# Attention stage of a two-layer tower: positional products copied out by ScalarE, and the score maximum of heads 4 to 7 moved into the exponential's bias

## The reference, cut to what matters

```python
# fourth block: 8 heads of 8 columns, per sequence
patch_score = softmax(einsum('bhnd,bhmd->bhnm', q, k) * hd**-0.5)
pos_score = softmax(rel @ Wpos.T + bpos)            # 8 x 128 x 128, the same for every sequence
g = sigmoid(gating)                                 # one number per head
attn = (1 - g) * patch_score + g * pos_score
attn = attn / attn.sum(-1)
h = h + (einsum('bhnm,bhmd->bhnd', attn, v) @ Wproj.T + bproj)
# fifth block: top-2 of 8 experts, softmax over the two logits
logits = xn @ Wr + br
y = sum_e w[e] * (gelu(xn @ W1[e] + b1[e]) @ W2[e] + b2[e])
```

## Time and profile before

| what | value |
|---|---|
| median of 3 runs | 781.05 us (781.04 to 781.59) |
| profiled execution, its own time | 780.1 us |
| its span | 778.4 us |
| granted TensorE clock, mean over the span | 0.899 of full |
| busy in the span: TensorE / VectorE / ScalarE | 81% / 61% / 35% |
| attention loop, first scores to first `expert_up` | 596.7 to 697.8 us |

### The profile page before, as it was taken

One profiled execution on the slowest core, in us unless ns is written; L12 is line 12 of the kernel. 1 busy time (PEld: TensorE's weight loads), 2 busy tenths in 40 slices (PEclk: granted clock), 3 DMA queues, 4 the chain that ended last, 5 costly groups with the idle time before them and its releaser, 6 DMA issues.

```text
span 778.4 us, 12091 instructions
## 1 busy us (share of the span) xinstructions
PE 630.4 (81%) x4557; PEld 483.8 (62%) x4557; DVE 476.8 (61%) x1164; ACT 272.2 (35%) x463; POOL 358.5 (46%) x406
## 2 busy tenths in 40 slices
PE   6779999999986637776877886459997779898996
PEld 3547767785565526666766765425776567774666
DVE  3775344247666757899889999844333746555513
ACT  0034454428965501110000000055332536645440
POOL 1576233218026666897888995134542200000324
PEclk9999999998988957899999999668995889898998
DMA  7000000000003330000000000000000000000000
GB/s 230 0 1 1 1 1 1 0 1 1 0 23 75 73 71 1 1 1 0 2 0 1 1 1 1 0 1 1 1 1 1 1 1 2 1 2 0 8 8 13
DMA packets 9689, 10.33 MB, mean 13 GB/s; under 512 B 5792, under 2 KB 8544, under 8 KB 9376
## 3 DMA queue, kind: packets, MB, share of 16 engines
q1 hardware_dynamic: 7584, 7.90, 3.7%
q0 software_dynamic: 2048, 1.68, 1.1%
HBM read 5.70 MB, written 0.52 MB: 8 GB/s over the span
## 4 chain that ended last, share of the span: by engine, by line
PE 53%; DVE 30%; issue 4%; POOL 4%; ACT 4%; DMA 3%; SPq 2%; DVEq 0%; POOLq 0%; ACTq 0%
PE bank L1242 8%; PE bank L992 7%; DVE features L1671 7%; PE bank L980 6%; DVE bank L1705 5%; DVE features L1694 5%; PE bank L1258 4%; PE bank L1260 4%; PE bank L1069 3%; PE bank L1029 2%; POOL rstd L336 2%; PE bank L1318 2%; DMA coefs<-xs 2%; PE bank L1038 2%; SPq L373 2%
## 5 line engine op out<-in xcount | busy, mean ns | idle before, releaser
L1069 PE MATMUL bank<-ident,features 128*128 128x128 f32 x920 | 126.6, 296 | 66.0 <-DVE features L1671 47.7
L1069 PEld LDWEIGHTS bank<-ident,features 128*128 128x128 f32 x920 | 113.4, 154 | 76.9 <-DVE features L1671 56.7
L495 POOL TENSOR_TENSOR features<-UV,coefs 128x1024 f32<-128x1024 f32 (+1 forms) x64 | 117.5, 1862 | 25.3 <-PE bank L1069 15.5
L1671 DVE TENSOR_TENSOR features<-UV,bank 128x1024 f32<-128x1024 f32 (+3 forms) x64 | 66.2, 1066 | 0.8
L668 ACT ACTIVATE G<-bank,cols 128x512 f32<-128x512 f32 x64 | 44.0, 687 | 59.5 <-PE bank L980 59.5
L980 PE MATMUL bank<-xs,weights 128*128 128x512 f32 x128 | 60.7, 619 | 1.8 <-ACT xs L659 1.8
L992 PE MATMUL bank<-weights,G 128*128 128x128 f32 x512 | 61.0, 278 | 0.0
L992 PEld LDWEIGHTS bank<-weights,G 128*128 128x128 f32 x512 | 59.7, 195 | 0.0
L343 POOL TENSOR_SCALAR rstd<-mv 128x4 f32<-128x4 f32 x8 | 1.5, 193 | 123.3 <-DVE mv L355 123.3
L1060 PE MATMUL bank<-features 32*128 32x136 f32 x768 | 36.1, 331 | 11.0 <-DVE xs L1626 5.1
L367 DVE TENSOR_SCALAR UV<-xs,mv,rstd 128x128 f32<-128x128 f32 x64 | 29.5, 561 | 25.0 <-POOL rstd L336 25.0
(11 more groups left out here) (301 smaller groups left out, 1359.3 us busy)
## 6 DMA issues: line engine op xcount, KB each, us to landing
weights<-in_w SPq DMA_DIRECT2D x2, 1024.0 KB, 8.3
weights<-in_ew SPq DMA_DIRECT2D x4, 256.0 KB, 3.9
features<-in_tok SPq DMA_DIRECT2D x1, 768.0 KB, 6.0
coefs<-G SPq DMA_DIRECT2D x16, 25.5 KB, 4.1
coefs<-G POOLq DMA_DIRECT2D x16, 25.5 KB, 4.1
coefs<-xs SPq DMA_DIRECT2D x16, 25.5 KB, 5.4
coefs<-xs POOLq DMA_DIRECT2D x16, 25.5 KB, 4.2
coefs<-weights POOLq DMA_DIRECT2D x16, 25.5 KB, 5.2
```

The costliest lines, as they stand in the source:

```text
L495: pool.tensor_tensor(out, u, co, ALU.mult).then_inc(s["held_p"], 1)
L1069: last = mm(out[:, P * k:P * k + P], x[:, P * k:P * k + P], ident[:], is_transpose=True, start=first and k == 0, stop=last_ and k == n - 1 ...
L1671: dve.tensor_tensor(out, u, co.unsqueeze(3).broadcast_to([P, R, NH, DH]), ALU.mult)\
```

## The change

- `normalise(t)`: for heads 0 to 3 nothing changes. For heads 4 to 7 VectorE takes only the maximum and multiplies it (128 x 4) by minus the scale. ScalarE then computes these four heads' exponentials straight from bank 3, one activation of 128 x 128 per head with that maximum as its bias, and raises the new semaphore `s_fold`; heads 0 to 3 follow in one activation of 128 x 512. `scores` of the next tile but one waits for `s_fold` as well as `s_sub`.
- `take_positions(c)`: ScalarE copies bank 1 to SBUF (`att2`), 128 x 256, at j = 0 of the next chunk. `mix` adds it, and `project_qk` waits for this copy (`pos_saved`) and no longer for `comb_done`.
- The positional probabilities are scaled by gate and total once, in `positional_softmax`, so `positional` needs eight columns and `mix` shrinks from eleven instructions to four.
- In the fifth block `router_exp(0)`, `save_weights(0)` and `turn_weights(0)` stand later, and VectorE does `mix(NC-1)` and `e_apply(NC-2)` ahead of `router_read(0)`, and `add_attended` and `e_stats` of the last chunk ahead of `router_weights(0)`.

```diff
 ScalarE
+            def take_positions(c):
+                act.wait_ge(s["pos_mm"], c + 1)
+                if c:
+                    act.wait_ge(s["comb_done"], c)
+                act.activation(att2.rearrange("p t (h d) -> p t h d", h=NH),
+                               bank[1][:, 0:CH * D].rearrange("p (h t d) -> p t h d", h=NH, t=CH),
+                               ACT.Copy).then_inc(s["pos_saved"], 1)
...
                 act.wait_ge(s["s_sub"], 2 * t + 2)
-                act.activation(sexp[:, t % 2], sexp[:, t % 2], ACT.Exp, scale=float(HD) ** -0.5).then_inc(s["s_exp"], 1)
+                for h in range(4, NH):
+                    last = act.activation(sexp[:, t % 2, h, :], bank[3][:, P * h - 512:P * h - 384], ACT.Exp,
+                                          bias=smax[:, t % 2, h:h + 1], scale=float(HD) ** -0.5)
+                last.then_inc(s["s_fold"], 1)
+                act.activation(sexp[:, t % 2, 0:4], sexp[:, t % 2, 0:4], ACT.Exp, scale=float(HD) ** -0.5).then_inc(s["s_exp"], 1)
                 if t and t % 2 == 0:
                     save_values_T(t // 2 - 1)
+                if j == 0 and c:
+                    take_positions(c - 1)
...
             save_values_T(T // 2 - 1)
+            take_positions(NC - 1)
             experts(1, 1)
-            router_exp(0)
             expert_gelus(1, 0, 0, 5)
             take_attended(NC - 1)
             expert_gelus(1, 0, 5, E)
-            save_weights(0)
+            router_exp(0)
             expert_gelus(1, 1, 0, 4)
             experts(1, 2)
             expert_gelus(1, 1, 4, E)
+            save_weights(0)
 TensorE, scores
                 if t:
                     pe.wait_ge(s["s_sub"], 2 * t)
+                    pe.wait_ge(s["s_fold"], t)
 TensorE, project_qk
                 if c >= 2:
-                    pe.wait_ge(s["comb_done"], c - 1)
+                    pe.wait_ge(s["pos_saved"], c - 1)
 TensorE, positional
-                    last = mm(bank[1][:, 36 * h:36 * h + 36], posT[:, h, :], vaug[c % 2][:, :, h, 0:HD + 1], start=True, stop=True)
+                    last = mm(bank[1][:, 32 * h:32 * h + 32], posT[:, h, :], vaug[c % 2][:, :, h, 0:HD], start=True, stop=True)
 TensorE, after the loop
             project_out(NC - 1)
-            turn_weights(0)
...
             expert_up(1, 1, 4, E)
+            turn_weights(0)
             second_bias(0)
 VectorE, positional_softmax
-                ch.settle()
-                ch(dve.reciprocal(comb[:, 0, 8:8 + NH], comb[:, 0, 0:NH]))
-                ch.settle()
-                tt(plog, plog, comb[:, 0, 8:8 + NH].unsqueeze(2).broadcast_to([P, NH, P]), mul).then_inc(s["p_done"], 1)
                 dve.wait_ge(s["gate_exp"], 1)
                 ch(dve.tensor_scalar(gate[:, 0, :], gate[:, 0, :], 1.0, None, plus))
...
+                ch(tt(share, total, inv, mul))
+                ch(tt(share, share, gate[:, 1, :], mul))
+                ch(tt(share, share, gate[:, 2, :], plus))
+                ch(dve.reciprocal(share, share))
+                ch(tt(f, inv, gate[:, 1, :], mul))
+                ch(tt(f, f, share, mul))
+                ch(tt(gate[:, 3, :], gate[:, 2, :], share, mul))
+                tt(plog, plog, f.unsqueeze(2).broadcast_to([P, NH, P]), mul).then_inc(s["p_done"], 1)
 VectorE, normalise
+                    if g:
+                        if t >= 2:
+                            dve.wait_ge(s["s_exp"], t - 1)
+                        ch(dve.tensor_reduce(m, x, AX_X, ALU.max))
+                        ch.settle()
+                        dve.tensor_scalar(m, m, -(float(HD) ** -0.5), None, mul).then_inc(s["s_sub"], 1)
+                        return
                     ch(dve.tensor_reduce(m, x, AX_X, ALU.max))
 VectorE, mix
                 dve.wait_ge(s["av_back"], 2 * c + 2)
-                dve.wait_ge(s["pos_mm"], c + 1)
+                dve.wait_ge(s["pos_saved"], c + 1)
...
                 ch(dve.reciprocal(cb[0], o[:, :, :, HD]))
-                ch(tt(cb[3], po[:, :, :, HD], g_, mul))
-                ch.settle()
-                ch(tt(cb[1], cb[0], omg, mul))
-                ch.settle()
-                ch(tt(cb[2], o[:, :, :, HD], cb[1], mul))
-                ch.settle()
-                ch(tt(cb[2], cb[2], cb[3], plus))
-                ch.settle()
-                ch(dve.reciprocal(cb[4], cb[2]))
-                ch.settle()
-                ch(tt(cb[1], cb[1], cb[4], mul))
-                ch(tt(cb[5], cb[4], g_, mul))
+                ch.settle()
+                ch(tt(cb[1], cb[0], keep_, mul))
                 ch.settle()
                 ch(tt(att.rearrange("p t (h d) -> p t h d", h=NH), o[:, :, :, 0:HD], cb[1].unsqueeze(3).broadcast_to(full), mul))
-                ch(tt(att2.rearrange("p t (h d) -> p t h d", h=NH), po[:, :, :, 0:HD], cb[5].unsqueeze(3).broadcast_to(full), mul))
                 ch.settle()
                 tt(att, att, att2, plus).then_inc(s["comb_done"], 1)
 VectorE, after the loop
+            mix(NC - 1)
+            e_apply(NC - 2)
             router_read(0)
-            e_apply(NC - 2)
-            mix(NC - 1)
-            router_weights(0)
             add_attended(NC - 1)
             e_stats(NC - 1)
+            router_weights(0)
+            e_apply(NC - 1)
             dve.wait_ge(s["w_ready"], 2)
             add_bias(0)
-            e_apply(NC - 1)
             weigh(0)
```

More of the change, by code:

```diff
@@ L273, in build @@
             p_rel p_sub p_exp p_done p_T p_evict gate_exp
-            d_norm d_T d_xT d_q d_qd d_k d_kcopy d_v d_vcopy s_mm0 s_mm1 s_sub s_exp s_T p_ready av_mm av_saved av_back pos_mm
+            d_norm d_T d_xT d_q d_qd d_k d_kcopy d_v d_vcopy s_mm0 s_mm1 s_sub s_fold s_exp s_T p_ready av_mm av_saved av_back pos_mm pos_saved
             comb_done at_T at_xT proj_mm d_add hb_ready
@@ L1906, in positional_softmax @@
                 dve.wait_ge(s["p_exp"], 1)
-                ch(dve.tensor_reduce(comb[:, 0, 0:NH], plog, AX_X, plus))
-                ch.settle()
-                ch(dve.reciprocal(comb[:, 0, 8:8 + NH], comb[:, 0, 0:NH]))
-                ch.settle()
-                tt(plog, plog, comb[:, 0, 8:8 + NH].unsqueeze(2).broadcast_to([P, NH, P]), mul).then_inc(s["p_done"], 1)
+                total, inv, share, f = (comb[:, 0, 8 * k:8 * k + 8] for k in range(4))
+                ch(dve.tensor_reduce(total, plog, AX_X, plus))
                 dve.wait_ge(s["gate_exp"], 1)
@@ L1914, in positional_softmax @@
                 ch.settle()
+                ch(dve.reciprocal(inv, total))
                 ch(dve.reciprocal(gate[:, 1, :], gate[:, 0, :]))
@@ L1967, in _ @@
             th = [P, CH, NH]
-            g_ = gate[:, 1, :].unsqueeze(1).broadcast_to(th)
-            omg = gate[:, 2, :].unsqueeze(1).broadcast_to(th)
+            keep_ = gate[:, 3, :].unsqueeze(1).broadcast_to(th)
             cb = [comb[:, k, :].rearrange("p (t h) -> p t h", t=CH) for k in range(6)]
@@ L1977, in normalise @@
                     dve.wait_ge(s[f"s_mm{g}"], t + 1)
+                    if g:
+                        if t >= 2:
+                            dve.wait_ge(s["s_exp"], t - 1)
+                        ch(dve.tensor_reduce(m, x, AX_X, ALU.max))
+                        ch.settle()
+                        dve.tensor_scalar(m, m, -(float(HD) ** -0.5), None, mul).then_inc(s["s_sub"], 1)
+                        return
                     ch(dve.tensor_reduce(m, x, AX_X, ALU.max))
-                    if t >= 2 and g == 0:
+                    if t >= 2:
                         dve.wait_ge(s["s_T"], 2 * (t - 1))
                     ch.settle()
-                    tt(sexp[:, t % 2, 4 * g:4 * g + 4, :], x, m.unsqueeze(2).broadcast_to([P, 4, P]), sub)\
-                        .then_inc(s["s_sub"], 1)
+                    tt(sexp[:, t % 2, 0:4, :], x, m.unsqueeze(2).broadcast_to([P, 4, P]), sub).then_inc(s["s_sub"], 1)
             def mix(c):
                 dve.wait_ge(s["av_back"], 2 * c + 2)
-                dve.wait_ge(s["pos_mm"], c + 1)
+                dve.wait_ge(s["pos_saved"], c + 1)
                 if c:
@@ L1991, in mix @@
                 o = bank[7][:, 0:CH * NH * 9].rearrange("p (t h d) -> p t h d", t=CH, h=NH)
-                po = bank[1][:, 0:CH * NH * 9].rearrange("p (h t d) -> p t h d", t=CH, h=NH)
                 ch(dve.reciprocal(cb[0], o[:, :, :, HD]))
-                ch(tt(cb[3], po[:, :, :, HD], g_, mul))
                 ch.settle()
-                ch(tt(cb[1], cb[0], omg, mul))
-                ch.settle()
-                ch(tt(cb[2], o[:, :, :, HD], cb[1], mul))
-                ch.settle()
-                ch(tt(cb[2], cb[2], cb[3], plus))
-                ch.settle()
-                ch(dve.reciprocal(cb[4], cb[2]))
-                ch.settle()
-                ch(tt(cb[1], cb[1], cb[4], mul))
-                ch(tt(cb[5], cb[4], g_, mul))
+                ch(tt(cb[1], cb[0], keep_, mul))
                 ch.settle()
```

## The result

The changed kernel takes 823.87 us (median of 4 runs, 822.47 to 825.02) against 781.32 for the kernel before in the same comparison: a ratio of 1.0537, 95% interval 1.0509 to 1.0565. I had said slower, and 800 us with a range from 785 to 816. The direction and the wait that I had named held; the price of the clock behind that wait did not, and the time lies above the range.

What follows compares the result with a forecast made beforehand. The chain was taken as mostly TensorE's (53%), with VectorE 30%. Serial waits +10.5, opening +2, later clock falls +9 and tail -2.7 made +18.8, so 800 us as a median, range 785 to 816.

Steps and rivals of the forecast that it cites:

- What releases the scores: Attention loop: scores of tile t+2 would also wait for ScalarE's folds of tile t+1, 1.5 to 2.9 us in nearly every loop.
- rival "faster": Scores' wait for `s_fold`: folds finish before TensorE's own loop work, so no new wait; 771.6 us, chance 0.07.
- The serial term, +10.5: Attention loop at full clock: scores wait in series behind ScalarE's copies and folds, 111.6 us against 101.1 measured before.
- five falls at 1.8: +9: Attention loop: idle stretches on TensorE bring five falls to 1.2 GHz at 1.8 us each, +9, ends 0 and 20.
- The opening: Start of the attention loop: half clock in both kernels, adding 2 us to the new full-clock sum.
- rival with half clock through much of the loop: Attention loop: every loop has its gap; with half the loop at 1.2 GHz the clock term is 25, 816 us, chance 0.12.
- The fold's price: ScalarE's 128 x 128 folds in the loop: 367 ns each, four done after 1.1 us, bounds 0.75 and 1.5.
- `mix` and the positional part: Attention loop: `project_qk` no longer waits for `mix`, removing two waits of 3.3 us.
- Positional softmax and the tail: Softmax: seven more VectorE instructions, 1.4 us, hidden in idle time, costing nothing. Behind the loop: -2.7 us, bounds -5.2 and 0.
- the 2.0 us that I had booked to that gap: Behind the loop: four products slowed to 5.66 us after TensorE's 3.21 idle would return to 3.62, -2.0 us.

Runs made afterwards that it cites:

- e2: The kernel before with the fold alone added: 824.42 us, ratio 1.0566 to the kernel before.
- e5: The kernel before with one more wait only, scores also waiting for ScalarE's one exponential of the preceding tile: 820.93 us, ratio 1.0579.
- e1: The changed kernel with the fold alone undone: 766.64 us, ratio 0.9861 to the kernel before.
- e4: The kernel before with only the new order behind the loop: 776.59 us, ratio 0.9983.
- e3: The changed kernel with ScalarE's folds moved ahead of the projection copies and the transposes' copies: 788.34 us, ratio 1.0134 to the kernel before.
- e6: The changed kernel with 5 to 11 unread products put in TensorE's waits per loop: 794.33 us, ratio 1.0222 to the kernel before.
- e8: The changed kernel without its fold, run again beside the positional part alone: 765.98 us, ratio 0.9854 to the kernel before.

## Why the prediction was right or wrong

- **What releases the scores.** Right. The new wait is for ScalarE's line in all fifteen places, and it was argued from ScalarE's program order, not from its 35% of busy time. The rival "faster" needed the folds to be ready before TensorE's own work ended, and no loop had that.
- **The serial term, +10.5.** Right in its steps: with the gaps filled, the loops that run at full clock take 7.64, 8.77, 5.70 and 7.62 where I had 7.5, 8.5, 5.4 and 7.4. They are 0.1 to 0.3 too short each, some 3 us over the loop.
- **The clock, "five falls at 1.8: +9".** This step failed. The loop spent 105 us at 1.2 GHz, and it is 150.0 - 111.6 = 38.4 us longer than my sum at full clock. Some 3.0 of these are the short steps above. The opening costs about 3.5, where I had 2 (its first two distances between scores take 13.3 us even in the filled kernel, and I had 9.8). About 32 are left for the later half clock, where I had 9, and 20 as an upper end. The number of falls was not the main miss: there were eight, as in that upper end. The clock stayed down for some 12 us each time on average, and a fall cost about 4 us, not 1.8. I had priced it by what it cost before (1.6), where TensorE's work ran beside VectorE's and the gaps did not come back. Here a gap stands in every loop, so the clock rises for a few microseconds and falls again, and all of TensorE's part of a loop is in the serial path: half clock costs 1.4 us at j = 2 (7.06 against 5.70) and 4.6 at j = 1 (13.34 against 8.77). My rival with half clock through much of the loop, at a chance of 0.12, is what happened. But it was priced at 816 for half of the loop, not for 70%.
- **The fold's price.** Right (387 ns against 367), and nearly without effect: between e2 and e5 the loops differ by 0.9 us. The Trainium skill's "ScalarE: Activation LUTs", section "What ACT_TABLE_LOAD costs", gives a longer one, an estimate of 0.386 us for 128 columns with a pointer; the 387 of this trace agrees with it (the prediction's 0.29 leaves the pointer out, which its 1.26 for four includes). Four folds take 1.16 us in loop 9, nearer to my 1.1 than to that 1.26.
- **`mix` and the positional part.** Right: no wait of `project_qk` is left, and alone the positional part takes 6.7 to 10.1 us off the loop, where I had 6.7 for the two waits. In the changed kernel the gain could not be seen; that it lay under the new waits is argued, not shown.
- **Positional softmax and the tail.** The softmax cost nothing that can be seen. The tail gave 2.6 in this profile where I had 2.7, with its terms: the 3.2 gap gone, four products at 3.72, then a stall of 1.74 (predicted 1.8) for the table loads. That it came so close is partly luck: with the same new order e1 and e4 gave 1.1, and e3 and e6 lost 5.5, and in each of these four the clock fell behind the loop, which it did not in the changed kernel until 819 us. The load cost 1.28 here again, with 0.01 us to the next instruction; the 2.66 of the Trainium skill's section named above is not what this trace shows.
- **Sum.** 48.9 = 10.5 (serial) + 3.0 (steps too short) + 3.5 (opening) + 31.9 (later half clock) in the loop, less 2.6 behind it, less 2.7 ahead of it that belong to no part of the change: 43.6 between the spans, 42.55 between the medians. The two terms of the clock are estimates from the distances of the filled kernel.

## What to carry to other kernels

Before moving work to an engine with much idle time, look at where in its program the work will stand and who waits for it: a release that hangs behind a queue of copies is in series with all that they wait for, however cheap it is. Here one wait cost 5.8%. A gap that recurs in every iteration should be priced with TensorE's whole part of the iteration at half clock (here for 70% of the loop), not as a few single falls. And a bundle of edits should be timed apart: two of the three parts here were together a gain of 1.5% that the third one hid.

## What the runs showed that I had not expected

Filling a wait with useless products made the changed kernel faster, though still 2.2% slower than the kernel before. Even two to four of them per loop, which leave TensorE standing part of each wait (23.1 us for the folds over the loop where it was 37.0), raised the mean clock in the loop from 0.65 to 0.85 and took 23.5 us off it.

The clock can fall in the midst of work without a gap. In e4, TensorE was busy from 692.80 on, behind 1.38 us of idle time, with the narrow products of `values_back` (36 columns) and `router` (8 columns) from 694.78 to 697.36. Five microseconds into this work it ran at 1.2 GHz:

```profile
694.00:696.00 2.00, 2.00 (x16) 1.00 0.00 0
696.00:698.00 2.00, 2.00 (x15) 0.95 0.00 0
698.00:700.00 2.00, 2.00 (x3) 0.50 0.00 0
```

The kernel before shows it once more, with no gap of over 0.1 us since 712.93 and the next chunk's `router` from 731.30 on:

```profile
730.00:732.00 2.00, 2.00 (x21) 1.00 0.03 8
732.00:734.00 2.00, 1.93 (x12) 0.86 0.00 0
734.00:736.00 2.00, 2.00 (x4) 0.50 0.00 0
```

The changed kernel has the same products at both places and stayed at 1.00. What makes the difference was not tried, and it is not in the program alone: e1 and e8 are one program, and at this place behind the start of the experts the clock fell in e1's profile and not in e8's. In the kernel before, half clock began 0.4 us into the idle time ahead of the third `expert_up`:

```profile
702.00:702.70 0.70, 0.37 (x4) 1.00 0.00 0
702.80:704.00 1.20, 0.00 (x0) 0.50 0.00 0
```

So the 2.0 us that I had booked to that gap are not shown to be owed to it.
